# Tokens on the partitions for the output projection, the FFN output, both residuals and the norms behind them

## The reference, cut to what matters

```python
def _ada_rmsnorm(x, t, gamma_w, beta_w):
    return (t @ gamma_w.T)[:, None, :] * _rmsnorm(x) + (t @ beta_w.T)[:, None, :]
# layer 0: 64 sequences of 64 tokens, 256 features, 16 heads of 16; t is the condition (64 x 64)
x = x + (t @ attn_alpha_w.T)[:, None, :] * _attention(_ada_rmsnorm(x, t, attn_gamma_w, attn_beta_w), W_q, W_k, W_v, W_o)
x = x + (t @ ffn_alpha_w.T)[:, None, :] * (silu(h @ gate_w.T) * (h @ hidden_w.T) @ out_w.T + out_b)
#   with h = _ada_rmsnorm(x, t, ffn_gamma_w, ffn_beta_w), 1024 hidden features
# layer 1
out = (x - mean) * rsqrt(var + 1e-5) * weight + bias
out = (out + tanh(t @ lin_w.T + lin_b)[:, None, :]) * weight + bias
```

## Time and profile before

| | us |
|---|---|
| median of 3 runs (lowest to highest) | 568.06 (567.49 to 570.94) |
| the profiled execution, its own time | 570.64 |
| its span in the trace | 568.5 |
| TensorE busy, share of the span | 519.0, 91% |
| weight loads (beside matmuls) | 395.9, 70% |
| VectorE | 436.0, 77% |
| ScalarE | 221.1, 39% |
| GpSimd | 191.8, 34% |

### The profile page before, as it was taken

One profiled execution on the slowest core, in us unless ns is written; L12 is line 12 of the kernel. 1 busy time (PEld: TensorE's weight loads), 2 busy tenths in 40 slices (PEclk: granted clock), 3 DMA queues, 4 the chain that ended last, 5 costly groups with the idle time before them and its releaser, 6 DMA issues.

```text
span 568.5 us, 11060 instructions
## 1 busy us (share of the span) xinstructions
PE 519.0 (91%) x4212; PEld 395.9 (70%) x4212; DVE 436.0 (77%) x791; ACT 221.1 (39%) x298; POOL 191.8 (34%) x132
## 2 busy tenths in 40 slices
PE   7965799999999999999999999999999999987991
PEld 3753577778776777678776777678776777665871
DVE  6678787478896788778895888778895887767656
ACT  2354353336333463336333553336333553222320
POOL 5002223254232623253232633263233632232330
PEclk9778999999999999999999999999999999998995
DMA  5293061002411050202310050202310040200021
GB/s 162 70 239 105 2 163 41 2 2 57 112 36 40 20 148 0 74 0 55 111 47 26 18 148 0 74 0 61 105 58 16 18 111 1 76 1 1 0 75 37
DMA packets 24937, 32.86 MB, mean 58 GB/s; under 512 B 2448, under 2 KB 18960, under 8 KB 24912
## 3 DMA queue, kind: packets, MB, share of 16 engines
q1 hardware_dynamic: 24912, 32.52, 21.1%
HBM read 17.77 MB, written 4.26 MB: 39 GB/s over the span
## 4 chain that ended last, share of the span: by engine, by line
PE 30%; issue 29%; DVE 20%; POOL 13%; DMA 3%; ACT 3%; SPq 1%; POOLq 0%; DVEq 0%; ACTq 0%
PE banks L544 11%; POOL hs L1192 7%; PE banks L555 6%; PE banks L501 4%; DVE nt L861 3%; POOL os L1179 3%; DVE work_c L975 2%; POOL x2s L1188 2%; PE banks L392 2%; DVE nt L857 2%; POOL xtok L1166 2%; PE banks L520 2%; DVE nt L863 1%; DVE nt L866 1%; DMA work_c<-xn 1%
## 5 line engine op out<-in xcount | busy, mean ns | idle before, releaser
L544 PE MATMUL banks<-x2s,gh 128*128 128x512 f32 x768 | 195.0, 402 | 4.3 <-DVE act_t L1014 3.7
L544 PEld LDWEIGHTS banks<-x2s,gh 128*128 128x128 f32 x768 | 141.6, 188 | 42.3 <-DVE act_t L1014 4.9
L1192 POOL TENSOR_TENSOR hs<-act_t,hs 128x512 fp32r<-128x512 f32 x64 | 83.3, 1302 | 133.7 <-ACT hs L730 133.7
L555 PE MATMUL banks<-hs,wout 128*128 128x512 f32 x384 | 102.5, 403 | 0.0
L555 PEld LDWEIGHTS banks<-hs,wout 128*128 128x128 f32 x384 | 70.0, 188 | 18.5 <-issue 3.5
L730 ACT ACTIVATE hs<-act_t 128x512 fp32r<-128x512 f32 x64 | 40.4, 631 | 95.0 <-DVE act_t L1018 92.8
L975 DVE RECIPROCAL work_c<-banks 128x512 f32<-128x512 f32 x16 | 53.6, 3352 | 23.8 <-PE banks L487 23.8
L1014 DVE SCALAR_TENSOR_TENSOR act_t<-act_t,banks 128x512 f32<-128x512 f32 x64 | 43.8, 684 | 32.0 <-ACT act_t L723 30.9
L723 ACT ACTIVATE act_t<-banks 128x512 f32<-128x512 f32 x64 | 37.7, 590 | 52.8 <-PE banks L544 52.8
L1179 POOL TENSOR_TENSOR os<-work_c,os 128x512 fp32r<-128x512 f32 x16 | 20.5, 1282 | 95.8 <-ACT os L743 95.8
L474 PE MATMUL banks<-qpair,kpar 64*128 64x128 f32 x512 | 49.9, 315 | 0.4 <-issue 0.4
(11 more groups left out here) (106 smaller groups left out, 680.0 us busy)
## 6 DMA issues: line engine op xcount, KB each, us to landing
xtok<-x_in SPq DMA_DIRECT2D x8, 512.0 KB, 3.7
qpair<-qT SPq DMA_DIRECT2D x32, 128.0 KB, 2.4
work_c<-xn SPq DMA_DIRECT2D x16, 256.0 KB, 3.7
xres<-xT_in SPq DMA_DIRECT2D x8, 512.0 KB, 4.7
shift<-shift_dram SPq DMA_DIRECT2D x16, 256.0 KB, 4.3
y<-final SPq DMA_DIRECT2D x7, 512.0 KB, 3.4
kpair<-kTb SPq DMA_DIRECT2D x32, 64.0 KB, 2.0
work_d<-ghT_in SPq DMA_DIRECT2D x2, 512.0 KB, 3.9
```

The costliest lines, as they stand in the source:

```text
L544: last = mm(banks[:, base + part, :], gh[:, a, k, w:w + P], x2s[:, b, k, :], start=(n == 0), stop=(n == 5))
L555: last = mm(banks[:, m, :], wout[:, a, c, P * m:P * m + P], hs[:, c % 2, b, :], start=(c == 0 and a == b == 0), stop=(c == CH - 1 and b == 1))
L1192: tt(hs[:, c % 2, 1, :], act_t[:, c % 2, :], hs[:, c % 2, 0, :].bitcast(F32), ALU.subtract)\
```

## The change

o_proj and ffn_out swap their operands: the activations are the stationary operand and the weights move, so the result has tokens on the partitions and comes as 24 and 12 matmuls of 256 columns instead of 12 and 6 of 512. out_b is added by two matmuls with a matrix of ones. alpha (for attention and FFN) and the final shift lie in DRAM as rows by sequence, and SP loads them for each group with every row repeated over its 64 token partitions (row_aa, row_af, shift). xres is x untransposed. The second norm's sums of squares are VectorE passes with a running sum, its inverse square root works on 128 x 4 values, and the normalised x2 is transposed by TensorE (transpose_x2). Square, square_sums, spread_rms, transpose_out and copy_x3 are gone. The layer norm's scaling is done by ScalarE (scale_x3), weight and shift by GpSimd. stats_x uses the same square passes. The transposed FFN tables shrink to gamma and beta, and in set-up VectorE builds the bias rows (setup_outb). In main(0) VectorE's fill(4) stands before normalise(0).

SP, the row tables:

```diff
+            def load_rows(dst, r, g, done):
+                for b in range(2):
+                    sp.dma_start(dst[64 * b:64 * b + 64, :, :],
+                                 rows_v[r][g][b:b + 1].to_broadcast([L, TT, D])).then_inc(done, 16)
+            def load_aa(g):
+                load_rows(row_aa, R_AA, g, ld_aa)
+            def load_af(f):
+                if later(f):
+                    sp.wait_ge(x3_steps, X3 * f)
+                load_rows(row_af, R_AF, f, ld_af)
...
             def step(i, first=False):
                 load_x(i + 1)
                 load_res(i)
+                load_aa(i)
+                load_af(i - 1)
```

TensorE:

```diff
             def o_proj(g):
+                def tile(t, ns):
+                    for n in ns:
+                        k, a, b = passes[n]
+                        last = mm(banks[:, 6 + t // 2, D * (t % 2):D * (t % 2) + D], os_[:, b, k, P * t:P * t + P],
+                                  wo[:, a, k, :], start=(n == 0), stop=(n == 5))
+                    return last
                 pe.wait_ge(o_hi, 2 * g + 2)
+                tile(0, range(4))
+                tile(2, range(4))
                 pe.wait_ge(o_lo, 2 * g + 2)
-                for m in range(KD):
-                    for n, (k, a, b) in enumerate(passes):
-                        last = mm(banks[:, 6 + m, :], wo[:, a, k, P * m:P * m + P], os_[:, b, k, :],
-                                  start=(n == 0), stop=(n == 5))
-                last.then_inc(op_mm, 1)
-            def square_sums(g):
-                pe.wait_ge(sq_ready, g + 1)
+                tile(0, range(4, 6))
+                tile(1, range(6)).then_inc(op_mm, 1)
+                tile(2, range(4, 6))
+                tile(3, range(6)).then_inc(op_mm, 1)
+            def transpose_x2(g):
+                if later(g):
+                    pe.wait_ge(h_steps, 2 * CH * g)
                 for t in range(TT):
+                    pe.wait_ge(x2n_scaled, TT * g + t + 1)
                     for k in range(KD):
-                        last = mm(banks[32 * t:32 * t + 32, 7, 0:P], cst[:, C_ONE:C_ONE + 32],
-                                  work_c[:, k, P * t:P * t + P], start=(k == 0), stop=(k == KD - 1))
-                last.then_inc(ss_mm, 1)
...
             def ffn_out(f, c):
+                if c == 0 and later(f):
+                    pe.wait_ge(x3_steps, X3 * f - 1)
+                if c == 0:
+                    for half in range(2):
+                        mm(banks[:, half, :], ones[:, :], outb[:, :, :].rearrange("p h n -> p (h n)"),
+                           start=True, stop=False)
                 pe.wait_ge(h_hi, CH * f + c + 1)
-                for m, a, b in ((0, 0, 0), (0, 1, 0), (1, 0, 0), (1, 1, 0), (0, 0, 1), (1, 0, 1)):
-                    if b and m == 0:
+                for a, b in ((0, 0), (1, 0), (0, 1)):
+                    if b:
                         pe.wait_ge(h_lo, CH * f + c + 1)
-                    last = mm(banks[:, m, :], wout[:, a, c, P * m:P * m + P], hs[:, c % 2, b, :],
-                              start=(c == 0 and a == b == 0), stop=(c == CH - 1 and b == 1))
+                    for t in range(TT):
+                        last = mm(banks[:, t // 2, D * (t % 2):D * (t % 2) + D], hs[:, c % 2, b, P * t:P * t + P],
+                                  wout[:, a, c, :], start=False,
+                                  stop=(c == CH - 1 and b == 1 and t % 2 == 1))
                 last.then_inc(out_mm, 1)
...
-                    square_sums(g - 1)
                 k_proj(g)
                 if not later(g):
                     q_proj(g)
+                if norm2:
+                    transpose_x2(g - 1)
                 if ln:
                     ffn_out(g - 2, CH - 1)
-                elif norm2:
-                    square_sums(g - 1)
                 v_proj(g)
-                if norm2:
-                    spread_rms(g - 1)
-                if ln:
-                    transpose_out(g - 2)
```

ScalarE, main:

```diff
+                if fed:
+                    feed(f, 0)
+                    place_v_swapped(g)
+                    for c in range(1, 4):
                         feed(f, c)
...
-                odd = 4 if fed else 2
-                exp(g, 0)
-                fill(4 if fed else 3)
-                exp(g, 1, odd)
-                if not fed:
...
+                    exp(g, 0)
+                    tanh(f, 4)
+                    exp(g, 1)
+                    hidden_hi(f, 4)
+                    if ln:
+                        scale_x3(g - 2)
+                    exp(g, 2)
+                    tanh(f, 5)
+                    exp(g, 3)
+                    o_split(g, 0)
+                    hidden_hi(f, 5)
+                    tanh(f, 6)
+                    o_split(g, 1)
+                    hidden_hi(f, 6)
...
-                exp(g, 2)
-                if not fed:
-                    exp(g, 3, odd)
-                o_split(g, 0)
-                fill(5)
-                if fed:
-                    exp(g, 3, odd)
-                o_split(g, 1)
-                fill(6)
```

VectorE:

```diff
+            def square_sum(x, scratch, total, done):
+                V.tensor_tensor_reduce(out=scratch, in0=x, in1=x, scale=1.0, scalar=0.0, op0=ALU.mult, op1=ALU.add,
+                                       accum_out=total).then_inc(done, 1)
...
             def residual1(g):
-                dve.wait_ge(op_mm, g + 1)
+                dve.wait_ge(ld_aa, 32 * g + 32)
                 dve.wait_ge(ld_res, 16 * g + 16)
-                V.tensor_tensor(by_seq(work_b[:, :, :]), by_seq(banks[:, 6:8, :]), table(AA, g), ALU.mult)\
-                    .then_inc(x2_steps, 1)
-                dve.wait_ge(x2_steps, 2 * g + 1)
-                V.tensor_tensor(x2[:, :, :], work_b[:, :, :], xres[:, :, :], ALU.add).then_inc(x2_steps, 1)
+                if later(g):
+                    dve.wait_ge(x2_kept, g)
+                for half in range(2):
+                    tiles = slice(2 * half, 2 * half + 2)
+                    dve.wait_ge(op_mm, 2 * g + half + 1)
+                    V.tensor_tensor(x2[:, tiles, :], banks[:, 6 + half, :].rearrange("p (t n) -> p t n", t=2),
+                                    row_aa[:, tiles, :], ALU.mult).then_inc(x2_steps, 1)
+                    dve.wait_ge(x2_steps, X2 * g + 2 * half + 1)
+                    V.tensor_tensor(x2[:, tiles, :], x2[:, tiles, :], xres[:, tiles, :], ALU.add).then_inc(x2_steps, 1)
+            def stats_x2(g):
+                for t in range(TT):
+                    if t % 2 == 0:
+                        dve.wait_ge(x2_steps, X2 * g + t + 2)
+                    square_sum(x2[:, t, :], x2n[:, t, :], ss[:, 1, t:t + 1], x2_stats)
             def norm2(g):
                 v, y, t = (nt2[:, i, :] for i in range(3))
-                dve.wait_ge(ss_mm, g + 1)
-                V.tensor_scalar(v, banks[:, 7, 0:P], 1.0 / D, EPS_RMS, ALU.mult, ALU.add).then_inc(norm2_steps, 1)
+                dve.wait_ge(x2_stats, TT * g + TT)
+                V.tensor_scalar(v, ss[:, 1, :], 1.0 / D, EPS_RMS, ALU.mult, ALU.add).then_inc(norm2_steps, 1)
                 dve.wait_ge(norm2_steps, N2 * g + 1)
...
-            def scale_x2(g, bank=1):
-                dve.wait_ge(x2_gamma, g + 1)
-                dve.wait_ge(rb_mm, g + 1)
+                for t in range(TT):
+                    V.tensor_scalar(x2n[:, t, :], x2[:, t, :], nt2[:, 1, t:t + 1], None, ALU.mult)\
+                        .then_inc(x2n_scaled, 1)
+            def gamma_x2(g):
                 for k in range(KD):
-                    V.tensor_tensor(work_b[:, k, :], work_b[:, k, :], banks[:, bank, :], ALU.mult)\
-                        .then_inc(x2n_steps, 1)
-                for k in range(KD):
-                    dve.wait_ge(x2n_steps, 2 * KD * g + k + 1)
-                    V.tensor_tensor(by_token(work_b[:, k, :]), by_token(work_b[:, k, :]), table(BF, g, k), ALU.add)\
...
                 dve.wait_ge(out_mm, CH * f + CH)
-                dve.wait_ge(h_lo, CH * f + CH)
-                for m in range(KD):
-                    V.scalar_tensor_tensor(
-                        out=by_token(act_t[:, m, :]), in0=by_token(banks[:, m, :]), scalar=outb[:, m:m + 1],
-                        in1=table(AF, f, m), op0=ALU.add, op1=ALU.mult).then_inc(x3_steps, 1)
+                V.tensor_tensor(final[:, :, :], banks[:, 0:2, :].rearrange("p a (t n) -> p (a t) n", t=2),
+                                row_af[:, :, :], ALU.mult).then_inc(x3_steps, 1)
+                dve.wait_ge(x3_steps, X3 * f + 1)
...
                 if norm2_:
-                    norm2(g - 1)
+                    gamma_x2(g - 1)
                 if ln:
                     residual2(g - 2)
-                if norm2_:
-                    scale_x2(g - 1)
                 q_out(g)
...
                     for n in range(EARLY, EARLY + 2):
                         cut_lo(n)
                     finish_shift()
+                    setup_outb()
                 if more:
-                    stats_x(g + 1)
```

(35 more changed lines are left out.)

418 lines of the change are left out of this document (217 added, 201 removed).

## The result

The changed kernel takes **586.79 us** (median of 4 runs, 586.45 to 587.76) against 568.03 (567.49 to 570.94): ratio **1.032** (95% interval 1.029 to 1.035), slower. The forecast was 592, with a range of 560 to 601. The span of the profiled execution grew from 568.5 to 585.2, by 16.7 us. The sum had forecast 23.9.

A forecast was written before the change was run, and what follows sets the result against it. TensorE, busy 91% of the span, was taken to set the time. Span 568.5 + 13.8 (six groups) + 7.2 (clock) + 5 (set-up) + 3.3 (group 1 head) - 5.4 (tail) = 592.4; median 592 us, range 560 to 601.

The forecast's parts named there:

- the chain: VectorE's second-norm work before the x2 transposes: TensorE stands 4.95 us per group, head +2.7 against 20.4.
- The block on the second sum: GpSimd's subtraction for the next group's low part of x holds VectorE's second residual sum 2.1 us.
- the race: Whether GpSimd's low-part subtraction or VectorE's second sum starts first, a matter of 0.2 us.
- the square passes: Four VectorE passes for the second norm's sums of squares, taken at 0.5 us each, bounds 0.35 and 0.75.
- the second block: GpSimd's low-part subtraction for FFN tile 7 holds the second norm's small VectorE passes 1.2 us.
- the clock: Low TensorE clock after each group's stop: 1.2 us, bounds 0 and 1.7; +7.2 for six groups.
- what is saved elsewhere: The group outside its head: two TensorE waits go, bias and 256-column matmuls add; net -0.4 us.
- The rule of the Trainium skill: Weight loads overlap matmuls only in differing row groups; 60 more would cost 6.4 us per group; rival chance 0.02.
- the waits at the end: In the tail, waits before the last output projection go: -1.8 us.
- Set-up: Group 0: weight cuts and bias rows before the first normalise delay the second attention half; +5 us, bounds +3 and +8.
- The end: Tail around the last output projection: shorter chain, fewer waits, low clock, less transposing; -5.4 us in all.
- the chain keeps up: Rival: GpSimd does not hold VectorE's passes, head 19.3 us, no low clock; 561 or 557 us, chance 0.21.

The follow-up runs named there:

- Experiment 1: Changed kernel, but from group 2 on GpSimd zeroes the low part of x, except four columns, instead of subtracting: 563.3 us, ratio 0.988.
- the pair of kernels in section 5: Changed kernel with values before transposes, ScalarE reordered, x's low part on VectorE, old set-up order: 553.7 us; same without the old set-up order: 556.3 us.

## Why the prediction was right, and which terms were off

**Right: the mechanism.** The links of the chain came in the order forecast, with both blocks where they were expected. From the output projection's start, forecast against measured (the chain's times are ends):

| | forecast | measured |
|---|---|---|
| VectorE's first product starts | 2.3 | 2.2 |
| first sum, length | 1.1 | 0.98 |
| second sum ends | 7.5 | 7.5 |
| square passes end | 9.5 | 8.85 |
| hidden 7 ends | 10.9 | 10.2 |
| small passes end | 14.3 | 13.2 |
| transposes start | 14.85 | 13.72 |
| stop on TensorE | 4.95 | 3.73 |
| transposes to first gate matmul | 8.25 + 1.2 | 9.5 |

**The block on the second sum** was priced at 2.1 and is 2.2, with the race lost by 0.01 us. Experiment 1 shows that it is the block, and not the sum: 2.93 us beside the subtraction, 0.73 beside the two memsets. It agrees with the Trainium skill (SBUF — State Buffer, "Who interferes with whom"): a VectorE instruction with two SBUF inputs contends with a GpSimd instruction that reads SBUF, "not with one that only writes it".

**Too dear: the square passes.** I took 0.5 us and they come 0.35 us apart, the lower bound: 0.6 of the 1.1 us by which the chain is shorter. The rest is the second block (0.95 instead of 1.2) and shorter steps before and in the small passes. The row that I gave for passes with an operand in PSUM, L981 at 307.78, does not show what I read from it, since GpSimd is idle there; L1014 at 309.66, beside L1179 from 309.21 to 310.50, does, with 0.69. Whether a square pass can be blocked had no row before. It has one now, in the norm of the next x. VectorE:

```profile
361.28 1.29 DVE L943 CUSTOM_DVE_ANT_0 x2n<-xtok 128x256 f32<-128x256 f32 x1
```

GpSimd beside it:

```profile
361.00 1.29 POOL L1252 TENSOR_TENSOR hs<-act_t,hs 128x512 fp32r<-128x512 f32 x1 [3.42 <-ACT hs L751]
```

**Too cheap: the clock,** 1.2 against 1.5 to 1.6 us. The row that I priced it from held only half a stretch of work; by the upper bound, 1.7, it would have been nearer. In the two groups with 10.6 us from the transposes to the first gate matmul the clock cost 2.6, above that bound; in the first of them the granted clock was 0.50 from 270 to 276. The chain priced 1.1 too long and the clock priced too low offset each other in part, and that was luck.

**Too cheap: what is saved elsewhere.** The rest of a group gained 0.84 instead of 0.4: the wait before the output projection was worth 0.3 and not 0.16, and 0.1 came from a shorter wait in the second gate matmul. The 256-column matmuls cost what the value projection said: 12 of them 1.50 to 1.54 from start to start, where six of 512 took 1.49 to 1.51. The weight loads stay hidden. The rule of the Trainium skill that I weighed against this (TensorE: Matmul & The Clock Gate, "The mechanism") is not what this trace shows; I left out that the same section also has a load pulled ahead when it targets the background weight buffer. The list of TensorE's work in the prediction adds up to -1.0 us, not -1.1; the sum does not use it.

**Counted twice: the waits at the end.** I gave the tail -1.8 for waits that go before the last output projection, but 0.96 of it was already in the -0.4 of that group; only 0.8 was left. This put groups 6 to 7 1.0 too far down. On the other side their clock cost 1.1 us more than in most groups, which no row of before could tell.

**Set-up.** Forecast +5, of which the order was +4.2. The two executions show +2.8, the pair of kernels in section 5 2.6 for the order. In VectorE's and TensorE's timelines of group 0 after:

```profile
53.18 3.35 DVE L1020 RECIPROCAL work_c<-banks 128x512 f32<-128x512 f32 x1
```

```profile
57.41 1.93 PE L520 MATMUL banks<-pt,cst 128*32 128x512 f32 x8 [5.76 <-DVE work_c L1026]
```

The normalisation starts at 53.18, not at 54.5: the loads did not queue up as feared, and the bias rows hide in waits (they end at 39.76, and the norm's small passes start at 45.69 where they started at 46.15).

**The end.** -2.8 against -3.6. The chain from the last output projection took 15.1 (forecast 16.1, before 17.5), but TensorE then waits 0.50 and 0.66 for the split of x2, where it waited 0.25 and 0.31.

In sum: six intervals 13.5 instead of 19.2, set-up 2.2 less, tail 0.8 more. Of the rivals, the one on the other side (the chain keeps up) fell by the two blocks that I had put against it. It was not far: with the first block and the low clock gone, the order of TensorE's head turned round and the old set-up order, the same change is worth -2.8%.

**Left open.** Why the same stop of 2.63 us brings the low clock in one group and not in the next. Why the first output projection moves by up to 3.7 us between kernels with the same set-up order. Whether the remaining waits of 0.45 and 0.88 can be filled, the second by keeping GpSimd's subtraction off the queries' passes.

## What to carry to other kernels

When work moves from the engine that is the bound to another one, write out the chain that the bound then waits for, with what every other engine does at each of those microseconds; a price from an undisturbed row is too low by whole instructions where GpSimd reads beside VectorE. Count a stop of the bound engine as its length plus what the clock costs behind it, and ask first whether work that needs nothing from the chain stands behind the stop: moving 2.9 us of it in front, with ScalarE's order to match, was worth 4% here, as much as taking away the larger of the two blocks with its clock. Before reordering, list every condition of the waiting instruction, the banks it writes among them.

## What the runs showed of the hardware

- A VectorE pass over 128 x 4 values took 1.11 to 1.15 us beside GpSimd's 128 x 512 subtraction, against 0.16: the price of a block is what is left of the other engine's instruction, even for so small a pass.
- Two VectorE passes from 128 x 512 float32 to bfloat16, each with one tensor input in SBUF, took 2.01 us beside GpSimd's subtraction, against 0.88.
- The same GpSimd buffer written without reading (two memsets of 0.52 us) left the 128 x 512 sum at 0.73.
- A square pass with a running sum over 128 x 256 float32 values takes 0.41 us and 0.35 from start to start; reading the sum, 0.08, lies beside the next pass.
- One stop of 2.63 us was followed by a granted clock of 1.00 in one group and of 0.61 over 4 us in another, with the same work before and behind it.
